# Five row tiles in rotation, earlier x loads, attention batches written out, and experts split per batch

## The reference

```python
# layer 0: one of 4 experts for each batch
top1 = argmax(x.mean(axis=1) @ router_w + router_b)
out  = adj @ (x @ expert_w[top1])
y    = relu(batch_norm(out))        # mean and variance over all batches of one expert
x1   = layernorm(x + y)
# layer 1: 16 heads of 32, bias 2*adj
a = softmax((x1 Wq^T)(x1 Wk^T)^T * 512**-0.5 + 2 * adj)     # rows of zeros give 0
out = layernorm(x1 + (a (x1 Wv^T)) Wo^T)
```

## Time and profile before

| | |
|---|---|
| time, median of 3 runs | 2429.72 us (2426.78 to 2431.78) |
| profiled execution, its own time | 2437.01 us |
| its span, first to last instruction | 2435.4 us |
| busy share of the span: PE, ACT, DVE, POOL | 90%, 66%, 64%, 13% |
| mean granted TensorE clock | 0.948 |
| layer 0, change of layer, layer 1 | about 0 to 389, 389 to 450, 450 to 2435 us |
| one pass of layer 1's loop, two batches | about 250 us |
| DMA, mean | 122 GB/s |

### The profile page before, as it was taken

One profiled execution on the slowest core, in us unless ns is written; L12 is line 12 of the kernel. 1 busy time (PEld: TensorE's weight loads), 2 busy tenths in 40 slices (PEclk: granted clock), 3 DMA queues, 4 the chain that ended last, 5 costly groups with the idle time before them and its releaser, 6 DMA issues.

```text
span 2435.4 us, 48543 instructions
## 1 busy us (share of the span) xinstructions
PE 2191.6 (90%) x14627; PEld 1737.5 (71%) x14627; DVE 1565.0 (64%) x3998; ACT 1614.9 (66%) x3529; POOL 317.0 (13%) x662
## 2 busy tenths in 40 slices
PE   5999996799898889888988898889899988989896
PEld 4888885577776677677766676777677766777774
DVE  6667766367666566656665657575757675757575
ACT  4554553578676668676766676677767776767675
POOL 2000001011111111101110202020202020202011
PEclk8999998899999999999999999999999998999999
DMA  6444342868585758575858586667667676666672
GB/s 240 140 155 152 123 139 104 113 95 154 96 148 94 133 95 149 99 133 104 141 103 138 106 134 110 123 106 137 106 123 121 114 131 110 120 108 123 111 107 55
DMA packets 147523, 297.77 MB, mean 122 GB/s; under 512 B 12978, under 2 KB 13010, under 8 KB 147154
## 3 DMA queue, kind: packets, MB, share of 16 engines
q1 hardware_dynamic: 135954, 256.96, 56.5%
q0 software_dynamic: 11328, 37.76, 5.9%
HBM read 110.12 MB, written 50.33 MB: 66 GB/s over the span
## 4 chain that ended last, share of the span: by engine, by line
PE 55%; issue 21%; DMA 14%; DVE 6%; ACT 1%; POOL 1%; SPq 0%; DVEq 0%; POOLq 0%; ACTq 0%
PE bank L606 22%; PE bank L652 15%; PE bank L636 8%; PE bank L621 7%; DMA z<-in_x_dram 6%; DMA out_dram<-z 4%; DMA adj_sb<-in_adj_dram 3%; DVE prob L1177 2%; PE bank L586 1%; DVE st_ln L1136 1%; PE bank L644 1%; DVE z L1149 1%; DMA qp<-stage_q 1%; ACT prob L891 1%; PE bank L578 0%
## 5 line engine op out<-in xcount | busy, mean ns | idle before, releaser
L1177 DVE CUSTOM_DVE_ANT_0 prob<-bank,adj_sb 128x512 f32<-128x512 f32 x1024 | 657.2, 685 | 140.5 <-PE bank L621 120.1
L891 ACT ACTIVATE prob<-prob,neg_max 128x512 f32<-128x512 f32 x1024 | 730.9, 722 | 14.7 <-DVE neg_max L1186 11.3
L771 ACT ACTIVATE probT<-bank 128x512 f32<-128x512 f32 x832 | 461.5, 593 | 361.5 <-PE bank L652 357.8
L652 PE MATMUL bank<-ident,prob 128*128 128x128 f32 x4096 | 565.4, 283 | 5.0 <-ACT probT L771 5.0
L652 PEld LDWEIGHTS bank<-ident,prob 128*128 128x128 f32 x4096 | 489.1, 145 | 107.9 <-issue 55.3
L621 PE MATMUL bank<-kp,qp 128*128 128x512 f32 x1024 | 359.4, 433 | 99.9 <-DVE row_max L1177 48.9
L1191 DVE COPY probT<-bank 128x512 f32<-128x512 f32 x192 | 131.9, 687 | 295.9 <-PE bank L652 249.7
L621 PEld LDWEIGHTS bank<-kp,qp 128*128 128x128 f32 x1024 | 180.8, 195 | 140.5 <-DVE row_max L1177 67.7
L636 PE MATMUL bank<-probT,v 128*32 128x256 f32 x4096 | 249.6, 384 | 0.5 <-issue 0.5
L606 PE MATMUL bank<-xT,wkT 128*128 128x512 f32 x768 | 211.5, 413 | 2.7 <-DVE z L1149 2.7
L606 PE MATMUL bank<-woT,oT 128*128 128x512 f32 x768 | 204.2, 402 | 0.0
(11 more groups left out here) (114 smaller groups left out, 2140.4 us busy)
## 6 DMA issues: line engine op xcount, KB each, us to landing
kp<-stage_k SPq DMA_DIRECT2D x256, 256.0 KB, 6.6
qp<-stage_q SPq DMA_DIRECT2D x256, 256.0 KB, 7.9
x_raw<-in_x_dram SPq DMA_DIRECT2D x16, 1024.0 KB, 7.1
adj_raw<-in_adj_t_dram SPq DMA_DIRECT2D x16, 1024.0 KB, 9.2
outT_spill<-outT SPq DMA_DIRECT2D x16, 1024.0 KB, 5.3
v<-outT_spill SPq DMA_DIRECT2D x16, 1024.0 KB, 11.3
z<-in_x_dram POOLq DMA_DIRECT2D x64, 256.0 KB, 4.0
adj_sb<-in_adj_dram SPq DMA_DIRECT2D x64, 256.0 KB, 7.9
```

Of the source, the lines that this page charges most:

```text
L652: ins = nc.tensor.transpose(t_bank[j % 2][:, mt * P:(mt + 1) * P], prob[:, s % 2, j, mt * P:(mt + 1) * P], ident[:, :])
L771: return nc.scalar.activation(dst, src, ACT.Copy, scale=scale)
L891: nc.scalar.activation(prob[:, s % 2, j, :], prob[:, s % 2, j, :], ACT.Exp, scale=2.0, bias=neg_max[:, s % 2, j:j + 1], accum_out=row_sum[ ...
L1177: nc.vector.tensor_tensor_reduce(prob[:, s % 2, j, :], s_bank[j][:, :], adj_sb[:, t, :], 1.0, LOWEST, ALU.add, ALU.max, row_max[:, g % 2, ...
```

## The change

- `z` gets five tiles. The four tiles of x1 of batch b+1, then the four of the residual of b, then x1 of b+2, and so on, take the next slot of five in turn (`x1_tile`, `residual_tile`).
- x loads go out at steps 2, 4, 5, 6. The first waits for x1 of b (long spilled), load t > 0 for the store of tile t-1.
- `spill_x1` and `load_x1` become four transfers of 256 KB each, still at steps 9 and 13.
- All 16 attention batches are written out; there is no loop and b is a constant.
- The experts stay whole (`expert`); in each batch ACT makes the high part of the chosen one and DVE the low part (`sel_low`, between z_low 0 and z_low 1). The splits at the start are gone; the first batch waits for all four experts to land.
- The attention weights pass one after another through one tile `w_raw` and are split behind batches 1 to 4 of layer 0, which are written out; the loop covers 5 to 14.
- The products of `score` go to PSUM; `score` also waits for `route`.

```diff
-X_LOADS = {s + 1: i for s, i in O_NORMED.items()}
+X_LOADS = {2: 0, 4: 1, 5: 2, 6: 3}
+def x1_tile(b, t):
+    return (NT * (2 * b - 2) + t) % (NT + 1)
+def residual_tile(b, t):
+    return (NT * (2 * b + 1) + t) % (NT + 1)
...
-            w_exp = [sb(l0, f"w_exp{p}", [P, E, NT, H], F32R) for p in range(2)]
-            raw = [sb(l0, f"w_raw{i}", [P, NT, H]) for i in range(4)]
+            expert = sb(l0, "expert", [P, E, NT, H])
+            w_raw = sb(l0, "w_raw", [P, NT, H])
...
-            z = sb(l1, "z", [P, NT, H])
+            z = sb(l1, "z", [P, NT + 1, H])
...
-        def iterations(eng, body):
-            body(0, 0, True, False)
-            with eng.Fori(0, B // 2 - 1) as i:
-                body(i * 2 + 1, 1, False, False)
-                body(i * 2 + 2, 0, False, False)
-            body(B - 1, 1, False, True)
+        def iterations(body):
+            for b in range(B):
+                body(b, b % 2, b == 0, b == B - 1)
...
             def load_x1(b, last):
-                sp.dma_start(z[:, :, :], rows(x1_dram, b)).then_inc(x1_back, 16)
+                sp.wait_ge(x1_spilled, 64 * (b + 1 if last else b + 2))
+                sp.wait_ge(xT_ps, NT * (b + 1 if last else b + 2))
+                for t in range(NT):
+                    if t == 0 or last:
+                        need(sp, out_stored[NT - 1 if t == 0 else t - 1], 16 * b)
+                    sp.dma_start(z[:, residual_tile(b, t), :], row_tile(x1_dram, b, t)).then_inc(x1_back, 16)
...
             def load_x(b, t, first):
-                if not first:
-                    wait_apart(pool, out_stored[t], 16 * (b - 1))
-                pool.dma_start(z[:, t, :], row_tile(x, b, t)).then_inc(x1_x_in[t], 16)
+                if t == 0:
+                    pool.wait_ge(x1_spilled, 64 * b)
+                    pool.wait_ge(xT_ps, NT * b)
+                else:
+                    need(pool, out_stored[t - 1], 16 * (b - 1))
+                pool.dma_start(z[:, x1_tile(b, t), :], row_tile(x, b, t)).then_inc(x1_x_in[t], 16)
...
             batch0(0)                       # ACT; DVE has sel_low and weight_low at the same places
-            with act.Fori(1, B - 1) as b:
+            for b in range(1, 5):
                 batch0(b)
+                weight_high(b - 1)
+            with act.Fori(5, B - 1) as b:
+                batch0(b)
...
+            def sel_low(b):
+                wait_apart(dve, route, 5 * b + 4)
+                no = dve.value_load(index8[0:1, 0:1], min_val=0, max_val=E - 1)
+                dve.wait_ge(sel_hi, b + 1)
+                tt(w_sel[1][:, :, :], expert[:, bass.ds(no, 1), :, :].rearrange("p o t n -> p (o t) n"),
+                   f32(w_sel[0][:, :, :]), ALU.subtract).then_inc(sel_lo, 1)
...
             def batch0(b):
...
-                z_low(b + 1)
+                z_low(b + 1, (0,))
+                sel_low(b + 1)
+                z_low(b + 1, (1, 2, 3))
...
             def add_residual(b, t, ps):
-                dve.wait_ge(x1_back, 16 * b + 16)
+                dve.wait_ge(x1_back, 64 * b + 64)
```

More of the change, by code:

```diff
@@ L186, in gnn_program @@
         experts_in = [sem(f"experts_in{e}") for e in range(E)]
-        experts_hi = sem("experts_hi")
-        experts_lo = sem("experts_lo")
-        raw_in = [sem(f"raw_in{i}") for i in range(4)]
+        raw_in = sem("raw_in")
         adj_in = sem("adj_in")
@@ L429, in _ @@
                 nc.gpsimd.memset(expert_no[:, e:e + 1], float(e)).then_inc(consts_made, 1)
[L431 to L436, removed]
+            pool.wait_ge(outT_ps, NT)
             for i, w in enumerate((WkT, WqT, WvT, WoT)):
-                pool.dma_start(raw[i][:, :, :], w.rearrange("(t p) n -> p t n", p=P)).then_inc(raw_in[i], 16)
+                need(pool, w_lo, i)
+                pool.dma_start(w_raw[:, :, :], w.rearrange("(t p) n -> p t n", p=P)).then_inc(raw_in, 16)
             pool.wait_ge(bn_chain, BN_VAR)
@@ L781, in adjT_high, with pick_expert @@
                 copy(adjT[0][:, :, :], adj_raw[:, :, :]).then_inc(adjT_hi, 1)
[L783 to L787, removed]
+            def pick_expert(b):
+                wait_apart(act, route, 5 * b + 4)
+                no = act.value_load(index8[0:1, 0:1], min_val=0, max_val=E - 1)
                 need(act, outT_ps, NT * b)
-                src = f32(w_exp[part][:, bass.ds(pick_expert.no, 1), :, :]).rearrange("p o t n -> p (o t) n")
-                copy(w_sel[part][:, :, :], src).then_inc(sel_lo if part else sel_hi, 1)
+                copy(w_sel[0][:, :, :],
+                     expert[:, bass.ds(no, 1), :, :].rearrange("p o t n -> p (o t) n")).then_inc(sel_hi, 1)
             def z_high(b, t):
@@ L798, in z_and_expert @@
                 z_high(b, 0)
[L799 to L803, removed]
+                pick_expert(b)
+                for t in range(1, NT):
+                    z_high(b, t)
             def copy_outT(b, tiles=range(NT)):
@@ L811, in copy_outT, with weight_high @@
                     copy(outT[:, t, :], out_bank[t % 2][:, :]).then_inc(outT_sb, 1)
[L813 to L815 removed]
+            def weight_high(i):
+                act.wait_ge(raw_in, 16 * i + 16)
+                m = "kqvo"[i]
+                copy(wT[m][0][:, :, :], w_raw[:, :, :], QSCALE if m == "q" else 1.0).then_inc(w_hi, 1)
             split_x(0)
             adjT_high(0)
[L819 to L825, removed]
+            for t in range(3):
+                z_high(0, t)
+            for e in range(E):
+                act.wait_ge(experts_in[e], 16)
+            pick_expert(0)
             z_high(0, 3)
[L827 to L830, removed]
             def batch0(b):
@@ L985, in score @@
                 need(dve, score_ps, b)
+                need(dve, route, 5 * b)
                 wait_apart(dve, x_added, 3 * b + 3)
@@ L1035, in _ @@
             sum_x(0)
-            z_low(0, (0,))
             dve.wait_ge(router_in, 16 * 2)
             score(0)
-            z_low(0, (1,))
+            z_low(0, (0,))
             pick(0)
-            expert_low(2, slice(0, NT))
-            z_low(0, (2,))
-            expert_low(3, slice(0, NT // 2))
+            z_low(0, (1, 2))
+            for e in range(E):
+                dve.wait_ge(experts_in[e], 16)
+            sel_low(0)
             z_low(0, (3,))
@@ L1065, in weight_low @@
                 if m == "q":
-                    ins = nc.vector.scalar_tensor_tensor(out=wT[m][1][:, :, :], in0=raw[i][:, :, :], scalar=QSCALE,
+                    ins = nc.vector.scalar_tensor_tensor(out=wT[m][1][:, :, :], in0=w_raw[:, :, :], scalar=QSCALE,
                                                          in1=f32(wT[m][0][:, :, :]), op0=ALU.mult, op1=ALU.subtract)
                 else:
-                    ins = tt(wT[m][1][:, :, :], raw[i][:, :, :], f32(wT[m][0][:, :, :]), ALU.subtract)
+                    ins = tt(wT[m][1][:, :, :], w_raw[:, :, :], f32(wT[m][0][:, :, :]), ALU.subtract)
                 ins.then_inc(w_lo, 1)
+            batch0(0)
+            for b in range(1, 5):
+                batch0(b)
+                weight_low(b - 1)
+            with dve.Fori(5, B - 1) as b:
+                batch0(b)
             chain = [0]
@@ L1089, in _ @@
             link(nc.vector.reciprocal(inv_cnt[:, :], inv_cnt[:, :]))
-            weight_low(0)
-            out_stats(B - 1, 0)
-            weight_low(1)
-            for i in range(1, NT):
+            for i in range(NT):
                 out_stats(B - 1, i)
```

71 lines of the change are left out of this document (24 added, 47 removed).

## The result

| | before | changed |
|---|---|---|
| time, median | 2430.75 us | 2257.93 us (2256.45 to 2262.85) |
| ratio | | 0.9295 (95% interval 0.9276 to 0.9314) |
| profiled execution / its span | 2437.01 / 2435.4 us | 2262.85 / 2261.1 us |

The forecast was 2253, the range 2225 to 2318. The busy shares (first part of the page): PE's share rose from 90% to 95%, with 55 us less of busy time for the same number of products, since fewer of them ran at half clock.

The account below looks back on a forecast made before the run. PE was taken to bound the kernel, through its idle and half-clock time. From 2437.0 us: -119 (step 9 stall), -52 (gaps), -12 (experts), +6 (weights) = 2260, less 7.3 to the median: 2253 us, range 2225 to 2318.

Parts of the forecast that it names:

- The stall at step 9: Layer 1, PE waits for add_y behind a late x load; five tiles and earlier loads save 119 us (58 to 135).
- The gaps: Layer 1, six issue gaps of PE between loop passes, about 9.5 us each; written-out batches save 52 us (40 to 58).
- each seam: Layer 1, ends of former passes: PE's 0.94 us wait for DVE behind an adj load was expected there after the change.
- transfers fill the gap: Rival, layer 1: k, q and adj transfers lose their catch-up pauses, half the step 9 gain returns, 2313 us; chance 0.18.
- x1 in four pieces: Layer 1, x1 spill and reload at steps 9 and 13: 0 us, at most 20 us if pieces land strictly one after another.
- Experts, start: Start of layer 0: score and chosen expert ready sooner, PE starts out of batch 0 at about 32; saves 12 us (4 to 14).
- Experts, later batches: Layer 0: DVE's low part of the expert just fits with 0.7 us to spare, 0 us; 34 us if not.
- The rival of a DVE-bound layer 0: Rival, layer 0: the 0.7 us to spare is too thin, DVE's extra work shows, 2287 us; chance 0.12.
- Weights: Layer 0, splits behind batches 1 to 4: DVE's late x_low and score cost 1.5 us a batch, +6 us (0 to 12).
- Change of layer: Between layers 0 and 1: weight splits had been under the batch norm chain, which stays; 0 us.
- The signs that I had named: L586 wait gone or under 15 us, issue gone, step 9 7 to 8 us, clock above 0.97, x loads 20 us before add_y.

Follow-up runs that it names:

- e1_straight: The kernel before with only its 16 attention batches written out: 2377.92 us (ratio 0.9779).
- e2_old_steps: The changed kernel with five z tiles kept but x loads back at steps 4, 5, 6, 8: 2326.10 us (ratio 0.9570).
- e12_relu_pairs: The changed kernel with attention weights' splits moved inside batches 1 to 4, adj first, x1 reload at step 11, relu copies at steps 2, 2, 3, 3: 2211.57 us.
- e3_layer0: The kernel before with only layer 0 changed (experts split per batch, weights through one tile behind batches 1 to 4): 2424.56 us (ratio 0.9983).
- e4_weights_in_gaps: The changed kernel with only the attention weights' splits moved inside batches 1 to 4 of layer 0: 2252.93 us (ratio 0.9268).
- e7_port: The changed kernel with one extra 128x2048 DVE subtraction put beside POOL's pow in the batch norm chain: 2261.26 us, run once.

## Why the prediction was right, point by point

The steps of layer 1 in the timelines of PE, each from the scores of one step to those of the next, summed over the batches; us saved against the kernel before. The last column is the kernel of 2211.6 us.

| steps | `e1_straight` | `e2_old_steps` | changed | `e12_relu_pairs` |
|---|---|---|---|---|
| 9 | 4 | 45 | 129 | 129 |
| 15 and 0 (end of a pass) | 58 | 59 | 57 | 57 |
| 1 to 3 | -17 | -17 | -29 | 14 |
| 4 to 8 | 12 | 12 | 12 | 11 |

- *The stall at step 9*, 119 us forecast, 129 measured: right, mechanism and size. 15.55 - 6.95 = 8.6 us in each of 15 batches. I had counted 14.5 batches and kept 1.1 us of wait for DVE; 0.6 us a batch was left.
- *The gaps*, 52 us forecast: the gaps themselves were 57, as priced at 9.5 each, and 53.5 came out with that edit alone. I took off 0.9 us for each seam, by the one row. That was the term most wrong: in the trace before, the seven seams inside a pass cost 0.1 to 4.2 us in steps 1 and 2, 1.9 in the mean, and in the changed kernel every batch has its late transfers. Steps 1 to 3 together lost 29 us, where I had 5.
- *So the rival "transfers fill the gap" did come*, with 29 us, 5 of them in my sum, against its 60. Taking away the gaps alone (`e1_straight`) lengthened step 2 by 21 us, and taking away the stall at step 9 lengthened it by 12 more. The order on SP's queue and ACT's place for relu decide whether it shows: with both changed the loss is gone. That the transfers had caught up during the pauses fits this; how the DMA engines share their time among them is not shown.
- *Steps 4 to 8*, not in my sum: 12 us gained, 5.9 of them one single wait in one batch of the profiled execution of before.
- *x1 in four pieces*, 0 forecast: right. The waits name the reload nowhere, at step 13 or 11. The Trainium skill's advice of transfers of at least 1 MiB (DMA: Bandwidth & Descriptors, Bandwidth) made no difference to the time that a run here shows: a piece of 256 KB landed in 8.4 us in the median, the whole in 11.3, and the reader came 30 us later. (The 7.9 us that I called a mean in this sum is a median.)
- *Experts, start*, 12 us forecast: 11.1. The wait for the score shrank from 8.8 to 1.9 us, and the one for the expert from 4.7 to 2.7. PE starts out of batch 0 at 32.35, where I had about 32. The start varies: `e3_layer0` and `e4_weights_in_gaps`, with the same start, have 31.07 and 30.89.
- *Experts, later batches*, 0 forecast: right, and thin. The low part ends at 218.3 and out starts at 218.72, 0.4 us to spare where I had 0.7. Behind the last weight PE waited for it once, 0.4 us. The rival of a DVE-bound layer 0 did not come.

```profile
216.02 2.29 DVE L995 TENSOR_TENSOR w_sel<-expert,w_sel 128x2048 fp32r<-128x2048 f32 x1 [1.72 <-ACT w_sel L770]
```
```profile
218.72 11.10 PE L542 MATMUL bank<-zT,w_sel 128*128 128x512 f32 x48
```

- *Weights*, +6 forecast: the four batches took 23.5 to 23.8 us (forecast 23.6) and the one behind them 22.8, 6.7 us in all; another 1.0 was lost in batch 0, before any weight. The size is right, and half of the mechanism. I followed only DVE, from `x_low` to the score, 1.3 us late, and it was. But PE was first held by ACT: its copy of out tile 0 stands behind the weight's and x's and adj's high parts, and PE, which needs that bank for out tile 2, waited 1.14 us there. That moved the score product itself, and the lateness that I had counted fell into the same time. By these rows either alone would cost nearly what both do, so that the size came out was luck.
- *Change of layer*, 0 forecast: 2.1 us gained, a port shared with POOL that I did not price.
- *The signs that I had named*: L586 behind `add_y` and the gaps of issue are gone, step 9 takes 6.95 us (7 to 8 forecast), the granted clock is 0.985 (above 0.97). The last x load leaves POOL only 13.6 us before its `add_y`, not 20, and that was enough.
- *Luck*: steps 1 to 3 lost 23 us more than the 5 forecast, step 9 and steps 4 to 8 gained 22 more. These errors cancel, and 2253 beside 2258 is nearer than its parts. The mechanisms of the two large parts are right without that luck.

## What to carry to other kernels

Price a stall by the distance between two rows of the bounding engine less its work at full clock; the wait alone was half of it. In an in-order queue look not only at when a transfer lands but at what stood ahead of it when it could have gone. When two engines wait side by side for two transfers, take both waits away before judging either edit: adj first gave 6 us alone and 26 us behind the later relu. And a price for a wait that recurs is a mean over all its places: one seam had 0.9 us, the seven had 1.9.

## What was not expected of the hardware

- Work that seemed hidden under a POOL operation lengthened it: pow of 16 columns took 2.94 us alone and 5.04 beside a DVE subtraction with two SBUF inputs (5.04 in the kernel before, `e1_straight` and `e7_port`, 2.94 in the changed kernel and four others).
- The score reductions into PSUM follow each other every 0.65 us, into SBUF every 0.61.
- In layer 1 behind the change the DMA engines were full for 21 us around a batch's start (share 1.01, 182 GB/s) while the mean share over 500 us was 0.73. A 1 MB load of v took 11.3 us to land in the median before, 14.7 with the batches written out and nothing else changed, and 15.4 in the changed kernel.
